# The last two attentions of a four-layer cross-attention kernel: attention outputs as products of high and low parts, values two steps ahead in shared places

## The chip, the cores and the metric

The kernel runs on one core of a Trainium2 chip. The metric is the device time of one execution in microseconds (us); lower is better.

## The reference

`x` is 8 x 256 x 256 (batch B=8, T=256 tokens, D=256), the context 8 x 64 x 256, all float32. Four cross-attention layers follow one another. The first three have small heads; the third ends in an MLP of width 1024. The fourth, called layer 3, holds two cross-attentions with 16 heads of K=128 and an MLP. Each of its attentions computes, with `h` the normalised `x`:

```python
qh = (h @ wq + bq).reshape(b, q_len, 16, 128)
kh = (kv @ wk + bk).reshape(b, 64, 16, 128)       # plus one more key row, bias_k
vh = (kv @ wv + bv).reshape(b, 64, 16, 128)       # plus one more value row, bias_v
weights = softmax(einsum('bqhk,bthk->bhqt', qh, kh) / sqrt(128))
x = x + einsum('bhqt,bthk->bqhk', weights, vh).reshape(b, q_len, 2048) @ wo + bo
```

After both, `x + gelu(layer_norm(x) @ w_fc1 + b_fc1) @ w_fc2 + b_fc2`.

## The kernel before

Each engine has its own hand-written instruction stream (functions `sync`, `tensor`, `vector`, `scalar`, `gpsimd`), and streams meet only at semaphores. A small class drops a wait whose value is already known to be reached on that engine. DMA loads are all issued by SyncE (SP), in order.

The two last attentions are one loop over steps, `STEPS` = -4 to 32. An attention is folded: since K=128 is as wide as the context is narrow, the kernel doesn't project queries. It multiplies the projected keys with wq, and the projected values with wo, per head. A tile is 128 tokens; there are 16 tiles in each attention, 32 in all, and `tile_of(j)` is tile j. Four tiles belong to a pair of batches, `n = j // 4`. Keys and values of a pair come in four quarters of four heads, `divmod(i, 4)`. In step j, quarter `j + 4` of the keys (`key_of`) and quarter `j + 3` of the values (`value_of`) are made, tile j gets scores and softmax, and tile j-1 its output. In even steps a later input is transposed.

TensorE (PE), in the order of a step: `key_projection` and `value_projection` (L866, from `project`), `tile_scores` (products of parts, L725 to L727), `key_products` (L943), `tile_transposed` of tile j-1 (L961), `value_products` (L979), `tile_output` of tile j-1 (L990), `tile_source` (L505, even steps). A float32 matmul is two records in the profile. "Products of parts": each float32 operand is held as a high part rounded to float32r and a low part, the rest; high x high, high x low and low x high are summed (`products`, L722). Scores already do so, outputs don't.

PSUM: the scores use two double banks, everything else four banks `work`, which change roles with each step (`step_banks`). A bank that holds value products in step j (third and fourth) is in step j+1 the one of the key projection (first) or value projection (second). `first_free` to `fourth_free` are the waits for that.

VectorE (DVE), in the order of a step: `value_bias` (L1486), in steps -4 to -1 `value_sums` (L1423), in steps 11 to 14 `wq_biased` (L1409), `tile_max_over` (L1502), `key_low` (L1494, two), `tile_shifted` (L1513), in steps 10 to 13 `wq_sums` (L1401), in even steps `tile_norm` (L1108), in steps 12 to 15 `value_sums` again, `tile_sums` (L1523 to L1527), in even steps `ln_finish` (L1118), `tile_residual` (L1533), in even steps `tile_source` (L1476, L1478), in steps -1 and 15 `value_constants` (L1539).

ScalarE (ACT): `key_bias` (L1899), `key_products` (high parts of the keys, L1909), `tile_out` of tile j-1 (transposed weights, L1929), `tile_exponentials` (L1922), `value_products` (L1917, plain float32 copies into `pv`). GpSimd (POOL): the statistics' small steps, the multiply of the exponentials by the reciprocals (L2166, after `tile_sums`), `wq_scaled` (L2141, after the multiply in steps 10 to 13), rows added to `x` (L2064). In step j, `wq_biased` waits for the `wq_scaled` of step j-1.

Keys live in 10 places of high and low parts, shared by quarter and batch, each used until its last tile's scores (`places_of_keys`). Values live in two buffers `pv`, one for each second pair. The keys' weights are streamed, 512 KB a step into two slots; the values' weights are loaded whole, four quarters an attention. `weight_high` (L1941, ACT) and `weight_low` (L2156, POOL) split the last MLP's weights in steps 28 and 29.

## Time and profile before

| | us |
|---|---|
| median of 3 runs | 1052.97 (1051.34 to 1053.47) |
| the profiled execution's own time | 1050.85 |
| its span | 1048.9 |
| PE busy | 983.2 (94%) |
| DVE busy | 710.6 (68%) |
| ACT busy | 515.1 (49%) |
| POOL busy | 402.8 (38%) |

The granted TensorE clock was 0.995 of full speed. The span runs from the first to the last instruction of the profiled execution; its own time holds 1.95 us more. A row of a timeline gives start, duration, engine, line, operation, output and input tiles, and in brackets how long the engine stood idle before it and what ended that. Busy times of PE are modelled and neighbours overlap, so spacings from start to start are the surer measure. PEld is the load of a matmul's stationary operand. The two attentions' loop lies between about 455 and 951 us of the span.

### The profile page before, as it was taken

What the parts mean: (1) busy time and instruction counts of PE and PEld (TensorE: products, weight loads), DVE (VectorE), ACT (ScalarE), POOL (GpSimd) and SP (SyncE); (2) the same over time, 40 slices, a digit from 0 to 9 for tenths busy, and PEclk for the clock granted to TensorE, in tenths of its full rate; (3) what the DMA queues carried; (4) which work ended last, traced back from release to release, by engine and by line L of the source; (5) the groups of instructions that cost most, each with busy time, mean ns of one, the idle gap of its engine ahead of it and who ended that gap; (6) DMA issues with size and microseconds to landing.
All of it is one profiled execution on the core that took longest, in us unless ns stands there. A gap on an engine that the chain in (4) does not pass through costs nothing.

```text
span 1048.9 us, 19279 instructions
## 1 busy us (share of the span) xinstructions
PE 983.2 (94%) x7764; PEld 829.5 (79%) x7764; DVE 710.6 (68%) x1199; ACT 515.1 (49%) x1028; POOL 402.8 (38%) x424
## 2 busy tenths in 40 slices
PE   6999999997998798988999999999999999989997
PEld 3667566555666798987898899889988899879997
DVE  4658999896788578645656667786566655675542
ACT  2557888777676544433333333333333433445542
POOL 2534689898876233100222213321222122362110
PEclk9999999999999999999999999999999999999999
DMA  9102000000000500041110024401110110200000
GB/s 328 61 1 81 1 2 1 2 1 2 1 1 1 207 15 1 1 139 43 42 41 32 30 82 141 140 22 41 41 39 23 41 41 2 81 1 11 22 21 31
DMA packets 23997, 47.57 MB, mean 45 GB/s; under 512 B 3938, under 2 KB 8804, under 8 KB 23268
## 3 DMA queue, kind: packets, MB, share of 16 engines
q1 hardware_dynamic: 23908, 46.34, 13.0%
q8 instruction: 61, 1.00, 0.4%
q14 instruction: 28, 0.23, 0.1%
HBM read 44.23 MB, written 2.10 MB: 44 GB/s over the span
## 4 chain that ended last, share of the span: by engine, by line
PE 72%; POOL 11%; DVE 9%; issue 4%; ACT 3%; DMA 0%; SPq 0%; POOLq 0%; DVEq 0%
PE work L990 10%; PE work L866 10%; PE work L979 5%; PE scores L725 5%; PE scores L727 5%; PE scores L726 5%; PE work L943 5%; POOL pair L2052 3%; PE work L725 3%; PE work L727 3%; PE work L726 3%; PE work L590 2%; PE work L961 2%; PE work L652 2%; POOL pair L2055 2%
## 5 line engine op out<-in xcount | busy, mean ns | idle before, releaser
L2011 POOL TENSOR_SCALAR stat<-stat 128x2 f32<-128x2 f32 (+1 forms) x49 | 11.1, 227 | 300.1 <-DVE stat L1112 298.8
L990 PE MATMUL work<-pair,probsT 128*128 128x256 f32 x512 | 119.1, 386 | 3.0 <-ACT probsT L1929 3.0
L866 PE MATMUL work<-ctxT,w 128*128 128x128 f32 x992 | 116.2, 275 | 3.3 <-DVE all_keys L1494 2.1
L866 PEld LDWEIGHTS work<-ctxT,w 128*128 128x128 f32 x992 | 114.5, 192 | 4.8 <-issue 4.0
L990 PEld LDWEIGHTS work<-pair,probsT 128*128 128x128 f32 x512 | 94.6, 190 | 26.3 <-issue 10.8
L1909 ACT ACTIVATE all_keys<-work 128x512 fp32r<-128x512 f32 x64 | 38.2, 597 | 143.1 <-PE work L943 143.1
L2166 POOL TENSOR_TENSOR probs<-probs,smax 128x1024 f32<-128x1024 f32 x22 | 42.0, 1909 | 139.0 <-DVE smax L1527 139.0
L1899 ACT ACTIVATE kvT<-work,cols 128x128 f32<-128x128 f32 x120 | 34.2, 368 | 106.0 <-PE work L866 106.0
L1502 DVE TENSOR_REDUCE smax<-scores 128x16 f32<-128x1024 f32 x32 | 39.1, 1222 | 53.9 <-PE scores L727 53.9
L725 PE MATMUL scores<-all_keys,src_l_high 128*128 128x256 f32 x256 | 74.5, 291 | 0.0
L727 PE MATMUL scores<-all_keys,src_l_low 128*128 128x256 f32 x256 | 71.7, 280 | 0.0
L726 PE MATMUL scores<-all_keys,src_l_high 128*128 128x256 f32 x256 | 71.6, 280 | 0.0
L979 PE MATMUL work<-w,kvT 128*64 128x256 f32 x512 | 62.3, 385 | 7.4 <-DVE all_keys L1494 7.4
L1174 DVE TENSOR_REDUCE smax<-scores 128x16 f32<-128x1024 f32 x48 | 58.1, 1210 | 11.6 <-PE scores L636 11.1
L1486 DVE TENSOR_TENSOR kvT<-work,cols 128x512 f32<-128x512 f32 x32 | 22.1, 690 | 63.5 <-PE work L866 63.5
L943 PE MATMUL work<-kvT,w 128*128 128x128 f32 x512 | 62.3, 275 | 0.0
L943 PEld LDWEIGHTS work<-kvT,w 128*128 128x128 f32 x512 | 59.8, 192 | 0.0
L979 PEld LDWEIGHTS work<-w,kvT 128*64 128x64 f32 x512 | 34.8, 136 | 25.9 <-issue 12.8
L1118 DVE TENSOR_SCALAR act_bufs<-x,stat 128x256 f32<-128x256 f32 x58 | 43.7, 796 | 16.1 <-POOL stat L2014 16.1
L2064 POOL TENSOR_TENSOR x<-x,rows_late 128x512 f32<-128x512 f32 x32 | 48.0, 1502 | 10.3 <-DVE act_bufs L1118 8.6
L2052 POOL TENSOR_TENSOR pair<-pair 128x512 f32<-128x512 f32 x32 | 41.3, 1289 | 27.2 <-ACT pair L1723 25.8
L1730 ACT ACTIVATE w<-work 128x512 f32<-128x512 f32 x88 | 47.3, 593 | 7.3 <-PE work L652 6.9
(198 smaller groups left out, 2802.8 us busy)
## 6 DMA issues: line engine op xcount, KB each, us to landing
w<-in_l_wk SPq DMA_DIRECT2D x32, 512.0 KB, 4.1
w<-in_l_wq SPq DMA_DIRECT2D x8, 512.0 KB, 5.9
w<-in_l_wo SPq DMA_DIRECT2D x8, 512.0 KB, 6.9
w<-in_l_wv SPq DMA_DIRECT2D x8, 512.0 KB, 4.3
x<-in_x SPq DMA_DIRECT2D x1, 2048.0 KB, 12.9
out<-x SPq DMA_DIRECT2D x8, 256.0 KB, 2.2
pair<-in_xT SPq DMA_DIRECT2D x1, 1536.0 KB, 7.1
pair<-in_l_fc SPq DMA_DIRECT2D x1, 1024.0 KB, 4.8
```

The lines of the kernel that those rows point to most:

```text
L725: mm(bank, s_hi, m_hi, start=start, stop=False)
L726: mm(bank, s_hi, m_lo, start=False, stop=False)
L727: return mm(bank, s_lo, m_hi, start=False, stop=stop)
L866: last = mm(bank[:, h * P:(h + 1) * P], w[:, c, h * K3:(h + 1) * K3], ctxT[:, c, p * P:(p + 1) * P], start=(c == 0), stop=(c == DC - 1))
L943: last = mm(step_banks(j)[2 + c][:, h * P:(h + 1) * P], w3_wq[:, 4 * g + h, c * P:(c + 1) * P], kvT[i % 2][:, h, :], start=True, stop=True)
L979: last = mm(bank[h * S:(h + 1) * S, bb * D:(bb + 1) * D], kvT[2][:, 2 * q + h, bb * S:(bb + 1) * S], w3_wo[:, 4 * g + 2 * q + h, :], start ...
L990: last = mm(step_banks(j + 1)[0][:, 0:D], probsT_bufs[j % 2][:, q, :], pv[n % 2][:, bb, q, :], start=(q == 0), stop=(q == GH // 2 - 1))
L1118: last = v.tensor_scalar(dst[:, t, :], src[:, t, :], st[:, 12 * t + 6:12 * t + 7], st[:, 12 * t + 9:12 * t + 10], ALU.subtract, ALU.mult)
L1174: v.tensor_reduce(smax[k % 2][:, 0:GH], s3, X, ALU.max).then_inc(d_max, 1)
L1730: act(pT[:, 4 * half:4 * half + 4, t, :], work[half][:, :].rearrange("p (q n) -> p q n", n=P), ACT.Copy).then_inc(a_pT, 1)
L2052: g.tensor_tensor(halves, e3[:, :, 0:n], e3[:, :, n:S], ALU.add).then_inc(p_half, 1)
L2064: g.tensor_tensor(xb(b), xb(b), row(name).unsqueeze(1).broadcast_to([P, TT, D]), ALU.add).then_inc(done, 1)
```

## The change

Each part as the code does it:

- `tile_output` uses products of parts. The transposed weights are held as high and low parts `pT_l3` in one buffer (before: whole, in two buffers), the values as high and low parts.
- Values get ten places of their own, assigned by the same function as the keys' places. Their high parts are written by ACT (`value_products`), their low parts by DVE (`value_low`, new). The low parts of the transposed weights are made by DVE (`tile_low`, new).
- Values are made two steps ahead, not three.
- The values' bias moves from DVE (one instruction) to ACT (four).
- The values' weights are streamed like the keys', a quarter at a time into two slots, 32 loads for 8.
- ACT copies values before the exponentials, not after. The last MLP's weights are split in steps 30 and 31 and lie elsewhere.

The pieces below come from the streams in this order: SP and PE, then DVE (`value_low`, `tile_low` and the loop), then ACT (`value_bias`, `value_products` and the loop).

```diff
         def value_of(j):
-            return j + 3 if 0 <= j + 3 < 8 * PAIRS else None
+            return j + 2 if 0 <= j + 2 < 8 * PAIRS else None
...
-            for i in range(4, 8 * PAIRS):
-                e.wait_ge(pe_kp, i - 1)
-                load_keys(i)
+            for i in range(2, 8 * PAIRS + 2):
+                if i < 8 * PAIRS:
+                    e.wait_ge(pe_kp, i - 1)
+                    load_quarter("k", i)
+                if i >= 4:
+                    e.wait_ge(pe_vp, i - 3)
+                    load_quarter("v", i - 2)
                 g = i - 2 - last
                 if 0 <= g < 4:
                     e.wait_ge(pe_pk, 2 * (last + g) + 2)
                     load_w3(2, g, "q")
-                if 1 <= g < 5:
-                    e.wait_ge(pe_pv, 2 * (last + g - 1) + 2)
-                    load_w3(2, g - 1, "vo")
+                if 2 <= g < 6:
+                    e.wait_ge(pe_pv, 2 * (last + g - 2) + 2)
+                    load_w3(2, g - 2, "o")
...
             def first_free(j):
                 e.wait_ge(d_mr, B)
                 e.wait_ge(d_kl, 2 * keys_before(j))
-                e.wait_ge(a_pv, 2 * values_before(j) - 1)
+                e.wait_ge(d_vl, 2 * values_before(j) - 1)
                 e.wait_ge(d_lr, tiles_before(j - 1))
             def second_free(j):
...
-                e.wait_ge(a_pv, 2 * values_before(j))
+                e.wait_ge(d_vl, 2 * values_before(j))
             def fourth_free(j):
...
-                e.wait_ge(d_vT, values_before(j))
-                e.wait_ge(a_lpT, 2 * tiles_before(j))
+                e.wait_ge(a_lv, values_before(j))
+                e.wait_ge(d_tl, 2 * tiles_before(j))
...
             def tile_output(j):
                 n, bb = j // 4, j // 2 % 2
-                e.wait_ge(a_lpT, 2 * j + 2)
-                e.wait_ge(a_pv, 8 * (n + 1))
                 for q in range(GH // 2):
-                    last = mm(step_banks(j + 1)[0][:, 0:D], probsT_bufs[j % 2][:, q, :], pv[n % 2][:, bb, q, :],
-                              start=(q == 0), stop=(q == GH // 2 - 1))
+                    e.wait_ge(d_tl, 2 * j + q // 4 + 1)
+                    e.wait_ge(d_vl, 8 * n + q + 1)
+                    k = value_at[PLACES[n, q // 2][bb]]
+                    last = products(step_banks(j + 1)[0][:, 0:D], [v[:, q, :] for v in pT_l3],
+                                    [all_values[:, k + part, q % 2, :] for part in range(2)], q == 0, q == GH // 2 - 1)
                 last.then_inc(pe_lo, 1)
...
-            def value_bias(i):
-                a, n, g = attention_of(i)
-                e.wait_ge(pe_vp, i + 1)
-                e.wait_ge(d_diff, 4)
-                e.wait_ge(pe_pv, 2 * i)
-                v.tensor_tensor(kvT[2][:, :, :], step_banks(i - 3)[1][:, :].rearrange("p (h s) -> p h s", h=4),
-                                col(f"l3_bv{a}", 4 * g, 4).unsqueeze(2).broadcast_to([P, 4, P]),
-                                ALU.add).then_inc(d_vT, 1)
+            def value_low(i):
+                for q in range(2):
+                    e.wait_ge(a_pv, 2 * i + q + 1)
+                    v.tensor_tensor(both_values(i, q, 1), step_banks(i - 2)[2 + q][:, :].rearrange("p (b d) -> p b d", b=2),
+                                    both_values(i, q, 0).bitcast(F32), ALU.subtract).then_inc(d_vl, 1)
+            def tile_low(j):
+                for half in range(2):
+                    high, low = (flat(p[:, 4 * half:4 * half + 4, :]) for p in pT_l3)
+                    e.wait_ge(a_lpT, 2 * j + half + 1)
+                    v.tensor_tensor(low, step_banks(j + 1)[half][:, :], high.bitcast(F32), ALU.subtract).then_inc(d_tl, 1)
...
             for j in STEPS:
-                if value is not None:
-                    value_bias(value)
                 if j < 0:
                     value_sums(1, j + 4)
                 if 11 <= j < 15:
                     wq_biased(2, j - 11)
                 if tile_of(j) is not None:
                     tile_max_over(j)
                 if key_of(j) is not None:
                     key_low(key_of(j))
+                if j == 4 * B:
+                    hidden_low(0, 0)
+                    last_affine(1)
+                    hidden_low(0, 1)
+                if tile_of(j - 1) is not None:
+                    tile_low(j - 1)
                 if tile_of(j) is not None:
                     tile_shifted(j)
+                if value_of(j) is not None:
+                    value_low(value_of(j))
...
+            def value_bias(i):
+                a, n, g = attention_of(i)
+                e.wait_ge(pe_vp, i + 1)
+                e.wait_ge(d_diff, 4)
+                e.wait_ge(pe_pv, 2 * i)
+                for h in range(4):
+                    last = act(kvT[2][:, h, :], step_banks(i - 2)[1][:, h * P:(h + 1) * P], ACT.Identity,
+                               bias=col(f"l3_bv{a}", 4 * g + h))
+                last.then_inc(a_lv, 1)
             def value_products(i):
-                a, n, g = attention_of(i)
-                slot_free(n, pe_lo, None)
+                e.wait_ge(d_mr, B)
+                e.wait_ge(pe_lo, PLACES[divmod(i, 4)][2])
                 for q in range(2):
                     e.wait_ge(pe_pv, 2 * i + q + 1)
-                    act(pv[n % 2][:, :, 2 * g + q, :],
-                        step_banks(i - 3)[2 + q][:, :].rearrange("p (b d) -> p b d", b=2), ACT.Copy).then_inc(a_pv, 1)
+                    act(both_values(i, q, 0), step_banks(i - 2)[2 + q][:, :].rearrange("p (b d) -> p b d", b=2),
+                        ACT.Copy).then_inc(a_pv, 1)
...
                 if key is not None:
                     if key >= 2:
                         key_bias(key)
+                if value is not None:
+                    value_bias(value)
+                if key is not None:
                     key_products(key)
...
+                if value is not None:
+                    value_products(value)
                 if tile_of(j) is not None:
                     tile_exponentials(j)
-                if value is not None:
-                    value_products(value)
-                if j in (4 * B - 4, 4 * B - 3):
+                if j in (4 * B - 2, 4 * B - 1):
                     for q in range(4):
-                        weight_high(j - 4 * B + 4, q)
+                        weight_high(j - 4 * B + 2, q)
```

## Rows read from the trace of the kernel before

**Rows 1.** The page's part 1, busy us, share of span, instructions.

```profile
PE 983.2 (94%) x7764; PEld 829.5 (79%) x7764; DVE 710.6 (68%) x1199; ACT 515.1 (49%) x1028; POOL 402.8 (38%) x424
```

**Rows 2.** Windows of steps 17 and 11: stretch, its length, busy times, clock, DMA.

```profile
743.00:757.60 14.60, 14.60 (x114) 13.20 (x114) 6.75 (x11) 5.35 (x11) 1.90 (x1) 1.00 0.11 36
646.00:661.00 15.00, 15.00 (x118) 13.55 (x117) 14.47 (x27) 5.36 (x11) 5.82 (x4) 1.00 0.43 141
```

**Rows 3.** Timeline of PE, from step 14's value products into step 15.

```profile
701.58 1.95 PE L979 MATMUL work<-w,kvT 128*64 128x256 f32 x16
703.46 3.72 PE L990 MATMUL work<-pair,probsT 128*128 128x256 f32 x16
707.02 0.60 PE L505 MATMUL work<-ident,act_bufs 128*128 128x128 f32 x4
...
710.95 0.37 PE L725 MATMUL scores<-all_keys,src_l_high 128*128 128x256 f32 x1
...
713.86 1.95 PE L943 MATMUL work<-kvT,w 128*128 128x128 f32 x16
```

**Rows 4.** Timeline of step 16, DVE and PE's outputs, to step 17's maximum.

```profile
729.08 1.22 DVE L1502 TENSOR_REDUCE smax<-scores 128x16 f32<-128x1024 f32 x1 [2.14 <-PE scores L727]
...
731.49 0.69 DVE L1494 TENSOR_TENSOR all_keys<-work,all_keys 128x512 fp32r<-128x512 f32 x1 [0.20 <-ACT all_keys L1909]
732.10 1.21 DVE L1513 TENSOR_TENSOR probs<-scores,smax 128x1024 f32<-128x1024 f32 x1
...
733.50 3.72 PE L990 MATMUL work<-pair,probsT 128*128 128x256 f32 x16
...
734.53 1.22 DVE L1523 TENSOR_REDUCE smax<-probs 128x16 f32<-128x1024 f32 x1 [0.26 <-ACT probs L1922]
...
739.36 0.69 DVE L1478 SCALAR_TENSOR_TENSOR src_l_low<-work,src_l_high 128x512 fp32r<-128x512 f32 x1
...
744.09 1.23 DVE L1502 TENSOR_REDUCE smax<-scores 128x16 f32<-128x1024 f32 x1 [2.12 <-PE scores L727]
```

**Rows 5.** Timeline of DVE, POOL and PE in steps 10 to 14.

```profile
638.36 1.22 DVE L1502 TENSOR_REDUCE smax<-scores 128x16 f32<-128x1024 f32 x1 [2.13 <-PE scores L727]
...
646.71 2.23 DVE L1118 TENSOR_SCALAR act_bufs<-x,stat 128x256 f32<-128x256 f32 x2
...
646.87 1.92 POOL L2166 TENSOR_TENSOR probs<-probs,smax 128x1024 f32<-128x1024 f32 x1 [0.58 <-DVE smax L1527]
...
648.75 2.41 POOL L2141 TENSOR_TENSOR w<-w,pair 128x1024 f32<-128x1024 f32 x1
...
651.19 2.30 DVE L1409 TENSOR_TENSOR w<-w,pair 128x1024 f32<-128x1024 f32 x1
653.41 1.21 DVE L1502 TENSOR_REDUCE smax<-scores 128x16 f32<-128x1024 f32 x1
...
667.96 1.22 DVE L1502 TENSOR_REDUCE smax<-scores 128x16 f32<-128x1024 f32 x1 [0.99 <-PE scores L727]
...
684.83 1.21 DVE L1502 TENSOR_REDUCE smax<-scores 128x16 f32<-128x1024 f32 x1
...
686.16 1.28 DVE L1494 TENSOR_TENSOR all_keys<-work,all_keys 128x512 fp32r<-128x512 f32 x2
...
686.99 1.95 PE L979 MATMUL work<-w,kvT 128*64 128x256 f32 x16 [1.39 <-DVE all_keys L1494]
...
698.23 1.23 DVE L1409 TENSOR_TENSOR w<-w,pair 128x1024 f32<-128x1024 f32 x1 [1.33 <-POOL w L2141]
699.37 1.22 DVE L1502 TENSOR_REDUCE smax<-scores 128x16 f32<-128x1024 f32 x1
```

**Rows 6.** The page's part 6, DMA issues: count, KB each, us to landing.

```profile
w<-in_l_wv SPq DMA_DIRECT2D x8, 512.0 KB, 4.3
```

**Rows 7.** Timeline of PE, the opening of step -2.

```profile
466.89 3.81 PE L866 MATMUL work<-ctxT,w 128*128 128x128 f32 x32
```

**Rows 8.** Timeline of PE, step 31's transposes.

```profile
934.44 1.09 PE L961 MATMUL work<-ident,probs 128*128 128x128 f32 x8 [1.46 <-POOL probs L2166]
```

More of the change, by code:

```diff
@@ L133, in build @@
         probsT_sb = sb("probsT", [P, GH, P])
-        probsT_bufs = [probsT_sb[:, 8 * i:8 * i + 8, :] for i in range(2)]
+        probsT_at = nc.sbuf_base - 4 * GH * P
         smax = [sb(f"smax{i}", [P, 48]) for i in range(2)]
@@ L379, in both_keys, with both_values @@
             return all_keys[:, a:b + 1:b - a, c, :].rearrange("p b (h k) -> p b h k", h=4)
+        def both_values(i, q, part):
+            first, second, _ = PLACES[divmod(i, 4)]
+            a, b = value_at[first] + part, value_at[second] + part
+            return all_values[:, a:b + 1:b - a, q, :]
         def attention_of(i):
```

124 lines of the change are left out of this document (54 added, 70 removed).

## The prediction

> **What bounds the kernel now.** I read the page first, then windows of one step each, then the PE and DVE timelines, and last the steps with extra work. A step is one of the 37 passes of the last attentions' loop (j = -4 to 32), named by the tile j whose scores it makes. PE is busy 94% of the span and DVE 68% [rows 1]. In an ordinary step PE is busy all of it and DVE about half; in step 11 DVE is busy 14.5 of 15.0 us [rows 2], and in step 13 PE waits 1.39 us for it [rows 5]. So PE bounds the ordinary steps, and DVE is close to it in steps 10 to 15. PE's order in a step, to be followed in the timeline: two projections (L866), scores (L725), key products (L943), transposes, value products (L979), outputs (L990) and, in even steps, an input's transposes (L505) [rows 3]. The steps open with L866, 0.43 after L505 has begun. From maximum to maximum an even step takes 15.02 us (729.08 to 744.09 [rows 4]) and an odd one 14.58; 29.60 for two.
>
> **The outputs on PE.** Eight full-width matmuls run from 703.46 to 707.02: 3.56 us [rows 3]. They become 24 part products of the form that the scores have, 128x128 by 128x256, and 24 of those take 710.95 to 713.86, 2.91 us [rows 3]. Gain 0.65 us a tile. Its lower bound is nothing, if parts cost as much as whole ones, its upper 0.74, if the 0.09 of the change of type were not paid. I take 0.65, since the row is of the same form. PE alone would so need 13.93 and 14.37 us, 28.30 for two.
>
> **What DVE gets.** Two subtractions for the output parts of the values (value_low) and two for the transposed weights (tile_low), less one bias add. The nearest row is a pair of key_low, the same shapes: 1.28 us for two (L1494 at 686.16 [rows 5]), a little less from start to start; I take 1.25, so 2.5 before the row sums end, and 0.6 off in front of the next maximum. In an ordinary even step DVE's last operation ends at 740.0, and the next maximum waits for PE till 744.09: 4.1 us free [rows 4]. Less 2.5, less 0.65 (PE comes earlier), plus a 0.26 wait for the exponentials which goes: 1.2 us stay free. So there it costs nothing, and the cover is the scores of the next step; without it each us would be lost once in two steps.
>
> **New waits.** (1) The next key projection waits for value_low's first half, whose bank it overwrites. Counted from the maximum's start: key_low ends at 3.0 (729.08 to 732.10), tile_low 4.25, the shift 5.5, first half 6.1, and 0.13 more to reach PE (686.16 and 0.69 against 686.99 [rows 5]): 6.25. PE opens the outputs at 4.4 (733.50 [rows 4]) and arrives 2.9 later: 7.3. Free: 1.1 us. Behind the wait stands all of PE. (2) The outputs wait for tile_low, done at 3.7 for the first half; PE is there at 4.4. (3) With values two steps ahead the last quarter of a pair is made in the step that first reads it. Its halves are wanted at 6.5 and 6.9 and done at 6.25 and 6.9: I take nothing, bounds 0 and 0.4 in each of 7 steps.
>
> **Edits at nothing, in ordinary steps.** ScalarE's bias, four instructions, lies between the value projection's end and the key products, about 2.3 us of cover; uncovered it costs 1.1 a step. The value weights' loads add 512 KB a step (36 GB/s becomes about 70; in step 11 141 GB/s stand beside a full PE [rows 2]); they are queued behind the key's on SP, leave after a value projection two steps before their use, 28 us, and land in 4.3 us [rows 6]; without that cover each would cost up to 4.3. The places are shared in the keys' pattern and free in time. The MLP's weight parts move from steps 28 and 29 to 30 and 31, under the last chain and the hidden layer.
>
> **Steps 10 to 15, the term that decides.** Here DVE also has wq_sums (1.6), wq_biased and value_sums (2.0), and wq_biased(j) waits for POOL, whose multiply and scaling start only after the row sums. So 2.5 us before the sums move POOL, wq_biased and the next maximum alike. Maximum 10 to 11: sums end at 646.71 - 638.36 = 8.35, now 10.85; POOL's two 4.3 (646.87 to 651.16) after 0.16; then wq_biased 2.2: 17.55, where PE's share is 14.4 [rows 5]. The same way from the other starts (653.41, 667.96, 684.83, 699.37), estimates: 11 to 12: 15.5; 12 to 13: 19.15; 13 to 14: 17.05; 14 to 15: 14.65, there DVE's own queue; 15 to 16: 15.85, since the one matmul on value_sum waits until these sums are done. Together 99.75. Before they were 729.08 - 638.36 = 90.7 [rows 4, 5]. So +9.0, where PE alone would have given -5.4. Each late maximum makes key_low late, and the value products wait for key_low, as they already did in step 13 (1.39 us at 686.99).
>
> One price there stands both ways in the rows: wq_biased takes 2.30 us beside a POOL operation and 1.23 without, where it had waited 1.33 us for POOL [rows 5]. By the Trainium skill (SBUF — State Buffer, "SBUF: two separate sides") a DVE operation with two SBUF inputs and a GpSimd one that reads SBUF exclude each other, and whichever starts first holds the port. By that rule wq_biased could win twice (steps 11 and 13) and the sum would be 2.2 us lower than mine, which keeps 2.2 us for it there.
>
> **Start and end.** Start: with no value work in step -3, key projection 2 waits only for key_low(1), at 464.9 instead of 466.89 [rows 7]: -1.9. In steps -2 to 0 the projections wait for value_low, but ScalarE then takes the values before the exponentials, and step 1 opens at 496.1 instead of 498.7; -3.1 at step 2's start, with its tile's 0.65. Bounds 0 and -5. End: from step 28 to the hidden layer 39.8 us before. Step 29 gets a projection and products (1.77 + 1.87), four outputs give 2.6 back, and tile_low now stands between a maximum and its shift, in a part where PE waits for POOL's multiply anyway (1.46 at 934.44 [rows 8]): +0.6, bounds -3 and +4.
>
> **Sum.** Start -3.1; steps 2 to 9, 8 x -0.65 = -5.2; maxima 10 to 16 +9.0; the 12 steps 16 to 27 -7.8; end +0.6. Together -6.5. The profiled execution took 1050.85 (its span 1048.9, 1.9 around it), so 1044.4; it lies 2.1 under the median of the three timed runs, 1052.97. Carried to the median: 1046.5.
>
> **Rivals.** (A) The forecast: PE gains, and half of it is given back in steps 10 to 15: 1046.5, by itself 1041 to 1051. Chance 0.50. (B) No pile-up: the extra work slips into DVE's idle time, as its busy sum allows (14.5 of 15.0 us in step 11, half in ordinary steps). Then 14.4 of the term goes: 1032. Against it: in-order waits on POOL, which busy sums don't show. Chance 0.15. (C) Slower: the bank release of wait (1). It has 1.1 us free, and four subtractions, two evictions and a shift stand in its chain. If each step's chain is longer by d, about 27 steps lose d - 1.1; from d = 1.43 the kernel is slower than before, at d = 1.75 it is 1064. For it: a second key_low already waits 0.2 for ScalarE [rows 4], and there are more such hand-overs now. Against: four of them make 0.8. Chance 0.12. (D) The pile-up is larger than 14.4, as late maxima also delay the inputs' sources and the last quarter of values in step 13, and it reaches on into steps 16 and 17: 20 to 25 of it leaves 1052 to 1057. Chance 0.20. (E) The change doesn't do what it says, outputs as parts cost as much as whole: 28 x 0.65 lost, 1064.7. Chance 0.03; the scores' rows speak against it.
>
> About 0.2% (2.1 us) can be told from no change here. Faster by more: A but for a sliver, B, a little of D: 0.66. Within: most of D's better half and a sliver of A: 0.16. Slower: C, E and the rest of D: 0.18. The range leaves out the far half of B, most of C, and E: 1034 to 1057.
>
> **What would show it.** Right: no L990-like full matmuls; output groups of 2.9 us; ordinary steps of 13.9 and 14.4 us, with PE full and DVE at about 11 us of 14; maxima 10 to 16 spread over some 100 us with PE waiting for key_low before the value products, 1 to 5 us at a time in steps 11 to 14; step 1 opening some 2.6 us earlier. Wrong: PE waiting for value_low before a key projection in every step (C), for tile_low before the outputs, maxima 10 to 16 in 86 us (B), or a projection waiting for a DMA.

## The result, and the profile after

| | before | after |
|---|---|---|
| median of 19 runs each, us | 1051.27 | 1047.32 (1044.67 to 1051.02) |
| the profiled execution's own time | 1050.85 | 1046.57 |
| its span | 1048.9 | 1044.8 |
| granted TensorE clock | 0.995 | 0.989 |

The ratio is 0.9966, 95% interval [0.9955, 0.9976]: the changed kernel is faster by 3.9 us. Of its 19 executions the eleven with a granted clock of 0.987 to 0.990 took 1044.67 to 1047.80 us and the eight with 0.983 or 0.984 took 1048.39 to 1051.02, and the profile below is of the first kind. The forecast time, 1046.5, is 0.8 under the median. Of the forecast gain of 6.5 only 3.9 to 4.1 came, though: the three timed runs of before from which it was carried had a median 1.7 us above that of the 19 runs since.

The page of the changed kernel, busy times, and the streamed values' weights, 32 loads where [rows 6] has 8:

```profile
PE 969.0 (93%) x8020; PEld 827.6 (79%) x8020; DVE 758.1 (73%) x1295; ACT 558.0 (53%) x1156; POOL 403.6 (39%) x424
...
w<-in_l_wv SPq DMA_DIRECT2D x32, 512.0 KB, 5.0
```

Against [rows 1], PE is busy 14 us less while the span is only 4.1 shorter: some 10 us of new idle time stand in it. The waits of PE say where (who waits for whom, us in total, times, longest):

```profile
PE work L989 <- DVE all_keys L1496: 12.1, 7, 3.0
...
PE work L876 <- DVE all_keys L1496: 6.2, 1, 6.2
...
PE work L735 <- DVE pT_l_low L1510: 5.1, 3, 2.5
```

The code has moved down by some lines: the projections are L876 (before L866), products of parts L735 to L737 (L725 to L727; those with `pT_l` as operand are the new outputs), key products L953, transposes L971, value products L989, the maximum L1517, `key_low` L1496, `value_low` L1502, `tile_low` L1510, `wq_biased` L1420, `wq_scaled` L2161. L989 in the first line is so the wait of the value products, not an output.

**Ordinary steps.** PE's timeline, openings of steps 5 to 8, and the window of steps 5 and 6 (length, then PE, PEld, DVE, ACT, POOL busy, clock, DMA share, GB/s):

```profile
567.84 3.74 PE L876 MATMUL work<-ctxT,w 128*128 128x128 f32 x32
...
582.22 3.74 PE L876 MATMUL work<-ctxT,w 128*128 128x128 f32 x32
...
596.16 3.74 PE L876 MATMUL work<-ctxT,w 128*128 128x128 f32 x32
```

```profile
567.84:596.16 28.32, 28.32 (x246) 26.34 (x245) 20.83 (x37) 13.46 (x30) 6.08 (x5) 1.00 0.24 76
```

14.38 and 13.94 us, 28.32 for two, where 28.30 was forecast. PE is busy all of it and DVE for 20.8 of 28.3. In step 16 DVE has 1.38 us free before step 17's maximum, where the prediction kept 1.2:

```profile
743.40 1.22 DVE L1517 TENSOR_REDUCE smax<-scores 128x16 f32<-128x1024 f32 x1 [1.38 <-PE scores L737]
```

An output is now the stretch between L735 at 508.28 and L876 at 511.20, 2.92 us, where it was 3.56 [rows 3]:

```profile
508.28 0.38 PE L735 MATMUL work<-all_values,pT_l_high 128*128 128x256 f32 x1
...
511.20 3.07 PE L876 MATMUL work<-ctxT,w 128*128 128x128 f32 x26
```

**Steps 10 to 16.** DVE's timeline, the first three and the last of the seven maxima (the brackets tell for how long DVE had been idle, and for what):

```profile
631.07 1.22 DVE L1517 TENSOR_REDUCE smax<-scores 128x16 f32<-128x1024 f32 x1 [5.28 <-PE scores L737]
648.52 1.21 DVE L1517 TENSOR_REDUCE smax<-scores 128x16 f32<-128x1024 f32 x1
663.48 1.22 DVE L1517 TENSOR_REDUCE smax<-scores 128x16 f32<-128x1024 f32 x1
...
729.03 1.23 DVE L1517 TENSOR_REDUCE smax<-scores 128x16 f32<-128x1024 f32 x1 [4.96 <-PE scores L737]
```

97.96 us from 10 to 16, against 90.7 before [rows 4, 5]; those between are at 682.24, 699.14 and 713.53. The chain that stretches them, step 10 into step 11, on three engines:

```profile
641.63 0.25 DVE L1542 RECIPROCAL smax<-smax 128x16 f32<-128x16 f32 x1
641.96 1.92 POOL L2186 TENSOR_TENSOR probs<-probs,smax 128x1024 f32<-128x1024 f32 x1 [0.58 <-DVE smax L1542]
643.85 2.43 POOL L2161 TENSOR_TENSOR w<-w,pair 128x1024 f32<-128x1024 f32 x1
646.23 1.28 POOL L2084 TENSOR_TENSOR x<-x,rows_late 128x512 f32<-128x512 f32 x1
646.31 2.29 DVE L1420 TENSOR_TENSOR w<-w,pair 128x1024 f32<-128x1024 f32 x1 [0.62 <-POOL w L2161]
...
650.59 1.95 PE L989 MATMUL work<-w,kvT 128*64 128x256 f32 x16 [2.52 <-DVE all_keys L1496]
```

Multiply and scaling on POOL, then `wq_biased` on DVE, then the maximum, `key_low`, and only then the value products, for which PE has waited 2.52 us. In this profile the clock stayed at 1.00 behind that wait. In four other profiles with the same code in these steps (f3, f4, g2 and h1 below) the 16 value products behind the waits of 2.5 us (step 11) and 2.8 us (step 13) took 3.3 to 3.6 us each time instead of 1.95, and the seven maxima spanned 99.0 to 99.4 us; in f2 they spanned 97.94, at full clock.

**Where the gain went.** How far each mark lies ahead of the same mark of before (us), and what was forecast:

| mark | before | after | ahead | forecast |
|---|---|---|---|---|
| maximum 10 | 638.36 | 631.07 | 7.3 | 8.3 |
| maximum 16 | 729.08 | 729.03 | 0.05 | -0.7 |
| step 28 opens | 900.07 | 892.35 | 7.7 | 7.1 |
| hidden layer begins | 939.64 | 934.88 | 4.8 | 6.5 |
| end of the span | 1048.9 | 1044.8 | 4.1 | 6.5 |

All that was won up to maximum 10 is gone at maximum 16, the next twelve steps win 7.7 again, and the last four steps give 3.0 back where 0.6 was forecast.

**The last four steps.** Timeline of step 31 in the changed kernel, and the window of its outputs:

```profile
926.03 1.09 PE L971 MATMUL work<-ident,probs 128*128 128x128 f32 x8 [0.27 <-POOL probs L2186]
926.47 1.22 DVE L1517 TENSOR_REDUCE smax<-scores 128x16 f32<-128x1024 f32 x1
927.65 4.97 POOL L2176 TENSOR_TENSOR w_low<-w,w_high 128x512 fp32r<-128x512 f32 x4
927.73 1.21 DVE L1519 TENSOR_SCALAR smax<-smax 128x16 f32<-128x16 f32 x1
928.86 1.28 DVE L1510 TENSOR_TENSOR pT_l_low<-work,pT_l_high 128x512 fp32r<-128x512 f32 x2
929.59 0.58 PE L735 MATMUL work<-all_values,pT_l_high 128*128 128x256 f32 x1 [2.47 <-DVE pT_l_low L1510]
...
934.88 0.41 PE L735 MATMUL scores<-src_high,w_high 128*128 128x256 f32 x1
```

```profile
929.50:934.80 5.30, 5.21 (x24) 5.21 (x25) 3.55 (x7) 3.35 (x6) 3.58 (x4) 0.50 0.00 0
```

Between the transposes and the outputs PE waits 2.47 us for `tile_low`, which stands behind the maximum and the small operation L1519; that one took 1.21 us instead of the 0.18 it takes elsewhere. Then the granted clock is 0.50, the lower level of 1.2 GHz, and the 24 products take 5.29 us instead of 2.92. From the transposes to the hidden layer it is 8.85 us, against 5.20 before (934.44 [rows 8] to 939.64). Whether the clock falls here changes from profile to profile, as the experiments show.

**The start.** The same happens in step -2; PE's timeline and a window:

```profile
465.01 5.25 PE L876 MATMUL work<-ctxT,w 128*128 128x128 f32 x32 [6.24 <-DVE all_keys L1496]
```

```profile
465.00:468.00 3.00, 2.99 (x14) 3.00 (x15) 1.71 (x4) 0.00 (x0) 0.00 (x0) 0.50 0.00 0
```

The projection starts at 465.0 (forecast 464.9), but with nothing left for PE in step -3 its two waits of 2.1 us have become one of 6.24, the clock is 0.50 behind it, and 32 matmuls take 5.25 us. Before, they took 3.81 [rows 7].

### The profile page after: what moved, and what is told of

Same layout as the page of the kernel before. It is cut to its first block, busy times and chain, and to the rows that moved or that the text cites. A ratio compares the mean times of both kernels' runs of the same rounds, so it can differ in the third digit from the quotient of the medians.

```text
span 1044.8 us, 20014 instructions
## 1 busy us (share of the span) xinstructions
PE 969.0 (93%) x8020; PEld 827.6 (79%) x8020; DVE 758.1 (73%) x1295; ACT 558.0 (53%) x1156; POOL 403.6 (39%) x424
## 4 chain that ended last, share of the span: by engine, by line
PE 64%; DVE 14%; POOL 13%; issue 5%; ACT 3%; DMA 0%; POOLq 0%; SPq 0%; DVEq 0%
PE work L876 9%; PE work L735 6%; PE work L737 5%; PE work L736 5%; PE scores L735 5%; PE scores L737 5%; PE scores L736 5%; PE work L989 5%; PE work L953 4%; POOL pair L2072 4%; PE work L600 2%; POOL pair L2075 2%; PE work L971 2%; PE work L662 2%; PE work L515 1%
## 5 line engine op out<-in xcount | busy, mean ns | idle before, releaser
L876 PE MATMUL work<-ctxT,w 128*128 128x128 f32 x992 | 117.7, 277 | 6.5 <-DVE all_keys L1496 6.2
L876 PEld LDWEIGHTS work<-ctxT,w 128*128 128x128 f32 x992 | 114.9, 194 | 7.5 <-issue 7.5
L1517 DVE TENSOR_REDUCE smax<-scores 128x16 f32<-128x1024 f32 x32 | 39.1, 1223 | 82.3 <-PE scores L737 82.1
L735 PE MATMUL work<-all_values,pT_l_high 128*128 128x256 f32 x256 | 76.2, 297 | 5.1 <-DVE pT_l_low L1510 5.1
L735 PE MATMUL scores<-all_keys,src_l_high 128*128 128x256 f32 x256 | 74.1, 290 | 0.0
L989 PE MATMUL work<-w,kvT 128*64 128x256 f32 x512 | 62.3, 385 | 12.1 <-DVE all_keys L1496 12.1
L737 PE MATMUL work<-all_values,pT_l_low 128*128 128x256 f32 x256 | 72.8, 285 | 0.0
L736 PE MATMUL work<-all_values,pT_l_high 128*128 128x256 f32 x256 | 72.8, 284 | 0.0
L737 PE MATMUL scores<-all_keys,src_l_low 128*128 128x256 f32 x256 | 71.7, 280 | 0.0
L953 PE MATMUL work<-kvT,w 128*128 128x128 f32 x512 | 62.8, 275 | 1.1 <-DVE x L1548 0.9
L735 PEld LDWEIGHTS work<-all_values,pT_l_high 128*128 128x128 f32 x256 | 49.2, 192 | 17.0 <-DVE pT_l_low L1510 17.0
L953 PEld LDWEIGHTS work<-kvT,w 128*128 128x128 f32 x512 | 59.9, 192 | 1.6 <-issue 1.1
L989 PEld LDWEIGHTS work<-w,kvT 128*64 128x64 f32 x512 | 34.6, 136 | 30.9 <-issue 10.7
L1935 ACT ACTIVATE all_values<-work 128x512 fp32r<-128x512 f32 x64 | 38.3, 598 | 31.7 <-PE work L989 31.7
```

Source lines behind the costliest of these rows:

```text
L735: mm(bank, s_hi, m_hi, start=start, stop=False)
L736: mm(bank, s_hi, m_lo, start=False, stop=False)
L737: return mm(bank, s_lo, m_hi, start=False, stop=stop)
L876: last = mm(bank[:, h * P:(h + 1) * P], w[:, c, h * K3:(h + 1) * K3], ctxT[:, c, p * P:(p + 1) * P], start=(c == 0), stop=(c == DC - 1))
L953: last = mm(step_banks(j)[2 + c][:, h * P:(h + 1) * P], w3_wq[:, 4 * g + h, c * P:(c + 1) * P], kvT[i % 2][:, h, :], start=True, stop=True)
L989: last = mm(bank[h * S:(h + 1) * S, bb * D:(bb + 1) * D], kvT[2][:, 2 * q + h, bb * S:(bb + 1) * S], w3_wo[:, 4 * g + 2 * q + h, :], start ...
```

## Experiments

Every one starts from the changed kernel. Ratios are against the kernel before as timed beside the experiment, with 95% intervals; its medians there were 1051.23 us (f1 to f4), 1051.30 (g1 to g4) and 1051.97 (h1 to h3).

### The bias product behind the low parts (f1_bias_late)

Theory: in steps 11 to 14 the chain POOL, `wq_biased`, maximum is the bound, since `wq_biased` stands in front of the maximum.

```diff
-                if 11 <= j < 15:
-                    wq_biased(2, j - 11)
                 if tile_of(j) is not None:
                     tile_max_over(j)
...
                 if value_of(j) is not None:
                     value_low(value_of(j))
+                if 11 <= j < 15:
+                    wq_biased(2, j - 11)
```

> The changed kernel with wq_biased of steps 11 to 14 moved on DVE from before the maximum to behind value_low. Theory (the pile-up is an order, not a shortage: the row sums, POOL's multiply and scaling, wq_biased and the maximum form one chain): the span between maxima 10 and 16 falls from 97.96 us to about 92 (intervals 14.7, 13.9, 17.5, 13.9, 15.9, 15.9), the kernel gets about 6 us faster than the changed kernel. Rival (DVE is simply full there, its work takes as long wherever it stands): the maxima keep within 2 us of 98, nothing gained.

Measured 1042.20 us, ratio 0.9911 [0.9896, 0.9927], 5.1 under the changed kernel. Its first maxima of that stretch, and PE's wait:

```profile
634.33 1.23 DVE L1517 TENSOR_REDUCE smax<-scores 128x16 f32<-128x1024 f32 x1 [5.29 <-PE scores L737]
648.87 1.22 DVE L1517 TENSOR_REDUCE smax<-scores 128x16 f32<-128x1024 f32 x1
662.86 1.23 DVE L1517 TENSOR_REDUCE smax<-scores 128x16 f32<-128x1024 f32 x1 [2.60 <-PE scores L737]
```

```profile
PE work L989 <- DVE all_keys L1496: 3.7, 4, 1.5
PE work L953 <- DVE x L1548: 2.5, 2, 2.1
```

The intervals are now 14.54 and 13.99 us, where they were 17.45 and 14.96, and the seven maxima span 93.36 (634.33 to 727.69): 4.6 us are back, of the 7.2 that the stretch had lost. PE's wait for `key_low` falls from 12.1 to 3.7, and DVE no longer waits for POOL at `wq_biased` (9.3 us before the move). A wait of the key products takes its place, 2.05 us in step 13: they wait for tile 11's residual (L1548), whose bank they overwrite, and that comes at the end of step 12, where DVE is busy for 16.99 of 17.49 us. So the position of this one operation is the cause of most of the 7.2 us. Measured against PE alone (three times 28.32, 84.96 us) the changed kernel's 97.96 lie 13.0 over, and 8.4 of that are left. Most of them stand in steps 12 and 14 (17.49 and 16.82 us), which DVE's own work fills: it is busy for 16.99 and 16.58 us of them.

A second effect of the move can be read off. Each `wq_biased` now takes 1.22 us, where two had taken 2.29 and 2.30 beside a POOL operation; that is 2.1 us less. But the small operation behind the maximum meets POOL instead, in three steps, and takes 0.69, 0.65 and 1.47 us for 0.17:

```profile
696.72 1.47 DVE L1519 TENSOR_SCALAR smax<-smax 128x16 f32<-128x16 f32 x1
```

DVE's busy time over the seven maxima stayed the same (82.5 us, before the move 82.2), so the gain is in the waits and not in this price.

### The low parts before the last maximum (f2_low_first)

```diff
+                if j == 4 * B - 1:
+                    tile_low(j - 1)
                 if tile_of(j) is not None:
                     tile_max_over(j)
...
-                if tile_of(j - 1) is not None:
+                if tile_of(j - 1) is not None and j != 4 * B - 1:
                     tile_low(j - 1)
```

> In step 31 tile_low of tile 30 stands on DVE before the maximum instead of behind it. Theory (the wait of 2.47 us before tile 30's outputs lets TensorE's clock fall to half, which doubles the time of the 24 products that follow): the outputs start about 1.5 us earlier, the clock stays at 1.0 and they take 2.9 us, so the hidden layer begins about 3.9 us earlier. Rival (only the wait counts): 1.5 us earlier, and the products still at half speed.

Measured 1046.32 us, ratio 0.9960 [0.9946, 0.9974]; the profile shows the step better than the medians do. PE in its step 31:

```profile
927.86 0.38 PE L735 MATMUL work<-all_values,pT_l_high 128*128 128x256 f32 x1 [0.97 <-DVE pT_l_low L1510]
932.67 0.36 PE L735 MATMUL scores<-src_high,w_high 128*128 128x256 f32 x1 [1.72 <-POOL w_low L2178]
```

The wait for `tile_low` is 0.97 instead of 2.47, the clock stays at 1.00, and PE is done with the outputs 5.2 us after the transposes' start (925.79). But the hidden layer then waits 1.72 us for POOL's low parts of its weights, which the slow outputs had covered. From transposes to hidden layer 6.88 instead of 8.85: 2.0 us less, not 3.9. These 2.0 can't be credited to the edit alone. f1 and h3 leave `tile_low` behind the maximum and have the wait of 2.46 and 2.47 us, but in their profiles the clock stayed at 1.00, and they too need 6.88 and 6.90; their hidden layer waits 0.21 and 0.25 us for POOL. At full clock POOL's split of the weights so ends this interval at 6.9 us with either order.

### Work for PE in the same wait (f3_filler)

```diff
+                if j == 4 * B - 1:
+                    for _ in range(10):
+                        mm(work[1][:, 0:P], ident[:, :], ones[:, :], start=True, stop=True)
                 if tile_of(j - 1) is not None:
                     tile_output(j - 1)
```

> Ten extra matmuls of ident by ones (2.2 us) into a free half bank stand on PE between tile 30's transposes and its outputs, where PE waits 2.47 us for tile_low; they take nothing away from the wait. Theory (idle time makes the clock fall): the outputs begin where they did but run at full speed, 2.9 us instead of 5.3; 2.4 us faster than the changed kernel. Rival (the clock falls in that stretch for another reason, such as a throttle of the whole core): outputs still at half speed, nothing gained.

Measured 1046.81 us, ratio 0.9951 [0.9933, 0.9970]. PE in step 31, and the window in which the outputs run:

```profile
928.80 2.40 PE L1091 MATMUL work<-ones,ident 128*128 128x128 f32 x20
931.45 0.39 PE L735 MATMUL work<-all_values,pT_l_high 128*128 128x256 f32 x1 [0.26 <-DVE pT_l_low L1513]
...
934.77 0.36 PE L735 MATMUL scores<-src_high,w_high 128*128 128x256 f32 x1 [0.19 <-POOL w_low L2179]
```

```profile
931.00:933.00 2.00, 1.74 (x15) 1.55 (x15) 2.00 (x3) 0.00 (x0) 2.00 (x2) 1.00 0.00 0
```

The outputs start as late as before, and they run at full clock. From transposes (927.87) to hidden layer 6.90 us, 1.95 less. So of the loss in this step about 2 us are the clock. That PE's idleness brings them about is not shown by this run: without extra work the same wait of 2.46 to 2.48 us was followed by 8.85 to 8.86 us in three profiles (the changed kernel's, g2, h1), 7.95 in f4, where the clock came back after about half of the outputs, and 6.88 and 6.90 in f1 and h3. The filler's 6.90 can be the filler's doing or such a draw.

### The values' sums late at the start (f4_sums_late)

The value sums of quarters 1 to 3, on DVE in steps -3 to -1 ahead of `key_low`, go to the end of step -3.

```diff
-                if j < 0:
-                    value_sums(1, j + 4)
+                if j == -4:
+                    value_sums(1, 0)
...
+                if j == -3:
+                    for q in range(1, 4):
+                        value_sums(1, q)
                 if j in (-1, 15):
```

> At the loop's start the value_sums of steps -3 to -1 move behind key_low, all to the end of step -3. Theory: key projection 2 no longer waits 2.0 us for a value_sums that stands ahead of key_low(1), and the clock falls later or not at all, so step 1 opens 3 to 4 us earlier than the changed kernel's 497.2. Rival (key_low there waits for POOL's statistics, and the later steps of the start wait for value_low anyway): step 1 opens within 1 us of 497.2.

Measured 1045.10 us, ratio 0.9941 [0.9928, 0.9953]. Its opening of step -2:

```profile
465.27 6.12 PE L876 MATMUL work<-ctxT,w 128*128 128x128 f32 x32 [4.28 <-DVE all_keys L1496]
```

PE waits 4.28 us instead of 6.24, but the clock falls behind this wait as well: the projection takes 6.12 us. From step -3's key products (457.26) to step 1 (497.23) it is 39.97 us, in the changed kernel 42.15 (455.04 to 497.19). That is 2.2 us, between the two numbers on record, and the clock hides a part of it: to the next key products the projection needs 5.96 us here and 5.08 in the changed kernel. Without the projection's own time 34.01 us are left for 37.07 (and 34.02 in g3, which has the same edit), so the order wins 3.1 us, as the theory had it.

### Only the high parts of the outputs (g1_high_only)

The low parts are made but not multiplied, so this kernel leaves their share of the outputs out. It shortens PE by 16 of 24 products a tile, to see which new wait comes first.

```diff
-                    last = products(step_banks(j + 1)[0][:, 0:D], [v[:, q, :] for v in pT_l3],
-                                    [all_values[:, k + part, q % 2, :] for part in range(2)], q == 0, q == GH // 2 - 1)
+                    last = mm(step_banks(j + 1)[0][:, 0:D], pT_l3[0][:, q, :], all_values[:, k, q % 2, :],
+                              start=(q == 0), stop=(q == GH // 2 - 1))
```

> The changed kernel, but PE makes of each tile's outputs only the high by high product: 8 matmuls for 24; all low parts are still made. (Left out: the low parts' share of the outputs.) PE alone would then need 12.0 and 12.5 us for an odd and an even step. Theory (the release of value_low's bank, 6.25 us after the maximum's start, comes next, 6.6 after a step's opening): ordinary steps settle at about 12.85 us odd and 13.2 even, some 26.0 for two against 28.3, and PE waits for value_low before the key projection. Rival 1 (the release has room for more than that): 24.5 for two. Rival 2 (DVE was already the bound of ordinary steps): 28 for two, nothing gained.

Measured 1027.36 us, ratio 0.9770 [0.9751, 0.9789]. PE's waits of that kind, and the opening of an ordinary step:

```profile
PE work L1001 <- DVE all_values L1502: 7.9, 16, 0.9
PE work L876 <- DVE all_values L1502: 7.3, 19, 1.2
```

```profile
732.27 3.81 PE L876 MATMUL work<-ctxT,w 128*128 128x128 f32 x32 [0.18 <-DVE all_values L1502]
```

Steps open at 732.27, 745.91 and 758.76: 26.49 us for two. That is 1.83 less than 28.32, where 16 products of 0.117 us less in each would give 3.7; waits (1) and (3) of the prediction have taken the other half. The projection waits for `value_low` 19 times, the outputs for the last quarter (here L1001) 16 times. In the changed kernel both are covered, by some 0.9 us a step (half of 1.83; the prediction had 1.1): a chain longer than that, and rival C would have begun.

### The streamed values' weights twice (g2_loads_twice)

```diff
                     load_quarter("v", i - 2)
+                    a, _, g = attention_of(i - 2)
+                    e.wait_ge(s_in[f"l3_wv_{i % 2}"], 16 * 2 * ((i - 2) // 2))
+                    nc.sync.dma_start(w3_wv[:, i % 2, :, :],
+                                      A[f"l3_wv{a}"].rearrange("p (c n) -> p c n", c=DC)[:, :, 4 * g * K3:(4 * g + 4) * K3]
+                                      ).then_inc(s_in[f"l3_wv_{i % 2}"], 16)
...
-                e.wait_ge(s_in[f"l3_wv_{i % 2}"], 16 * (i // 2 + 1))
+                e.wait_ge(s_in[f"l3_wv_{i % 2}"], 16 * (2 * (i // 2) + 1))
```

> Each streamed quarter of the values' weights from the third on is loaded twice, the second time after the first has landed; projections wait for both. Theory (loads are hidden two steps ahead): ordinary steps stay at 13.93 and 14.37 us, the time within 1 us of the changed kernel's. Rival (traffic or SP's queue costs something in each step): at least 0.1 us a step, 3 us together, with waits of PE for a DMA.

Measured 1046.61 us, ratio 0.9963 [0.9949, 0.9977], the changed kernel's own time. Two steps of it:

```profile
740.90:769.20 28.30, 28.30 (x246) 26.33 (x245) 20.81 (x37) 13.47 (x30) 6.04 (x6) 1.00 0.34 113
```

113 GB/s and 28.30 us, against 76 GB/s and 28.32 above. The second loads cost nothing, and no wait of PE for a load of these weights appears.

### The three moves together (g3_three)

f1, f2 and f4 in one kernel.

> wq_biased behind value_low, value_sums late at the start and tile_low first in step 31, together. Theory (three separate stretches, gains add up): -4.6 in steps 10 to 15, -2.2 at the start, -2.0 at the end, 8.8 us less than the changed kernel's 1047.3, about 1038.5. Rival (the end's gain goes to the wait for POOL's weight_low, which then decides when the hidden layer starts): about 1040.5.

Measured 1039.49 us, ratio 0.9886 [0.9866, 0.9905]: between the two numbers, and faster than both kernels by 11.8 and 7.8 us. Maxima 10 to 16 span 92.89 us (630.04 to 722.93), step 1 opens 39.29 us after step -3's key products, and the hidden layer still waits for POOL:

```profile
926.79 0.36 PE L735 MATMUL scores<-src_high,w_high 128*128 128x256 f32 x1 [1.68 <-POOL w_low L2181]
```

### The last weights split earlier (g4_four)

To take that last wait, three of the first weight's four low parts go ahead of POOL's multiply in step 30 (its high parts ahead of the exponentials; the lines for that, and those that leave them out at the old places, are not printed).

```diff
+                if j == 4 * B - 2:
+                    for q in range(3):
+                        weight_low(0, q)
                 if tile_of(j) is not None:
```

> As the three together, and ScalarE makes the high parts of w1 before the exponentials of step 30, POOL three of four low parts before its multiply there. Theory (the hidden layer waits 1.72 us for weight_low once tile_low comes first): that wait goes, 1.5 us less than the three, about 1037. Rival (POOL's port keeps DVE's small operations of step 30 waiting and its multiply comes later): no gain or up to 2 us slower than the three.

Measured 1040.75 us, ratio 0.9895 [0.9877, 0.9913]: no gain on g3, though the intervals overlap. The wait moved to the transposes, which need POOL's multiply, and the clock fell again:

```profile
921.62 1.09 PE L971 MATMUL work<-ident,probs 128*128 128x128 f32 x8 [1.91 <-POOL probs L2197]
...
923.69 0.58 PE L735 MATMUL work<-all_values,pT_l_high 128*128 128x256 f32 x1 [0.98 <-DVE pT_l_low L1510]
```

```profile
923.60:929.00 5.40, 5.31 (x25) 5.32 (x26) 4.20 (x7) 2.06 (x4) 0.92 (x1) 0.50 0.00 0
```

The outputs take 5.28 us here for 2.92 at full clock. From the last scores of step 31 to the hidden layer it is 9.55 us in g4 and 7.45 in g3 (from 919.42 and 919.34). Without the 2.4 us of the clock the two would be about level, an estimate from these rows. So POOL's late multiply, the rival's reason, takes back what the earlier split gives, and the rest of the loss in this profile is the clock.

### Work for PE in the start's wait (h1_start_filler, h2_three_filler)

```diff
+                if j == -2:
+                    for _ in range(24):
+                        mm(sc[1][:, 0:P], ident[:, :], ones[:, :], start=True, stop=True)
                 if key is not None and key >= 2:
                     key_projection(j, key)
```

> The changed kernel with 24 plain float32 matmuls of ones in front of step -2's key projection, into a score bank that nothing uses at that time (they add nothing to the result). They fill most of the 6.24 us in which PE waits there for the keys' low parts. Theory: the projection's 32 matmuls took 5.25 us because the clock had fallen to 0.50 in the wait; with PE kept at work the clock stays at 1.00 there, they take about 3.75, and step 1 opens about 1.5 us earlier (40.6 instead of 42.15 after step -3's key products). Median down by about 1.5, to 1045.8. Rival: the steps behind are set by DVE and ScalarE, so step 1 opens as before and the time stays.

Measured 1047.09 us, ratio 0.9953 [0.9930, 0.9976], which can't be told from the changed kernel's 0.9966. The timeline shows the difference:

```profile
457.24 3.74 PE L953 MATMUL work<-kvT,w 128*128 128x128 f32 x32
460.81 5.52 PE L1074 MATMUL scores<-ones,ident 128*128 128x128 f32 x48
467.21 3.81 PE L876 MATMUL work<-ctxT,w 128*128 128x128 f32 x32 [0.87 <-DVE all_keys L1499]
```

The projection starts 9.97 us after step -3's key products, as it did (455.04 to 465.01), and takes 3.81 us at a clock of 1.00. Step 1 opens at 497.96, 40.72 after the key products instead of 42.15: 1.43 us, as the theory had it. Here the other profiles bear the theory out. In all ten without it the clock fell behind the wait of 6.24 or 4.28 us, and the projection needed 5.0 to 6.5 us to the next key products (5.08 in the changed kernel's, 4.99 in f2, 6.53 in f1); with it, here and in the next kernel, 3.65. The rest of the way to step 1 was 27.1 us in each profile with the changed kernel's start. So the clock costs 1.3 to 2.9 us there, and the changed kernel's profile has nearly the least of it. All of this profile lies 2.2 us later from before this loop on (457.24 against 455.04), in a part that the edit doesn't touch; shifts of that size can hide 1.4 us in a median of eight.

The same in the kernel of the three moves, with 17 matmuls:

> The kernel of the three moves (keys' bias product late, values' sums late, the last low parts first), with 17 such matmuls in front of step -2's key projection. Theory: the clock holds there as well, and some 1.5 us go from the 39.3 us between step -3's key products and step 1: 1038.0. Rival: no change, 1039.5.

Measured 1038.45 us, ratio 0.9871 [0.9851, 0.9892], the lowest time here; 0.9886 was g3's ratio. Step 1 opens 38.17 us after the key products (457.04 to 495.21), 1.1 less than in g3; the medians differ by 1.0, and the intervals overlap. In step 30 of this profile the clock fell in the middle of the outputs, behind waits of only 0.78 and 0.98 us, where g3 has the same waits and kept 1.00.

### The values' bias back on DVE (h3_bias_dve)

```diff
+                if value_of(j) is not None:
+                    value_bias(value_of(j))
                 if j < 0:
                     value_sums(1, j + 4)
```

(and ScalarE's call taken out; `value_bias` is DVE's single instruction of before.)

> The changed kernel with the values' bias back on DVE, one instruction at the front of its step, as before the change. Theory: in ordinary steps DVE has over 1 us free and nothing changes; in steps 10 to 15, where DVE's own queue sets the maxima, 0.6 us a step comes back, about 3 for the 97.96 of maxima 10 to 16; at the start, DVE has the key sums too: up to 1. Together 1050 to 1051. Rival: wq_biased waits for POOL anyway, so the bias add slips into that wait and costs nothing: 1047.3.

Measured 1048.58 us, ratio 0.9971 [0.9955, 0.9987]. The intervals from maximum 10 to 15 are 17.46, 14.97, 18.75, 16.89 and 14.98 us, in the changed kernel 17.45, 14.96, 18.76, 16.90 and 14.39. Where DVE waits for POOL anyway the bias add costs nothing; only 14 to 15, DVE's own queue, grows by 0.59. The rival was right for steps 10 to 13. At the start it costs more: step 1 opens 45.10 us after step -3's key products (457.88 to 502.98) instead of 42.15, and 1.4 of these 2.95 are the clock, with a projection of 6.62 us. That part isn't the edit's: f1, f3, g1 and g2 have the changed kernel's start and about as slow a projection (6.1 to 6.5 us to the next key products, here 6.45). The bias add costs the other 1.6.

This kernel's step 31, like f1's, gave something that no edit was meant for. It has the changed kernel's code there and the same wait, but not its clock:

```profile
935.90 0.39 PE L735 MATMUL work<-all_values,pT_l_high 128*128 128x256 f32 x1 [2.47 <-DVE pT_l_low L1519]
...
939.23 0.36 PE L735 MATMUL scores<-src_high,w_high 128*128 128x256 f32 x1 [0.25 <-POOL w_low L2185]
```

```profile
935.80:939.20 3.40, 3.08 (x24) 2.88 (x25) 2.26 (x5) 1.43 (x2) 3.17 (x3) 1.00 0.00 0
```

From transposes (932.33) to hidden layer 6.90 us, to the hundredth what the filler gave.

## Why the prediction was right, and where it was off

**The outputs: right.** 2.92 us a tile for a forecast 2.91, and 28.32 for two steps where PE alone should need 28.30. Rival E is out.

**What DVE gets, and waits (1) to (3): right.** In step 16 the first half of `value_low` (735.14, from the row at 734.45 and one eviction of 0.69) is done 6.1 us after the maximum, as worked out; PE doesn't wait for it in ordinary steps, and g1 shows both slacks to be small and real. The 1.2 us that were to stay free on DVE were 1.38. Rival C had the right place and did not reach its price.

**Edits at nothing: right but for one.** g2 shows it for the loads. The bias on ScalarE is no cost, and h3 shows what it saves: 0.59 in the one interval that DVE's own queue sets, and 1.6 at the start. The edit that was not free is the move of the MLP's weight parts; it comes under the end.

**Steps 10 to 15: the mechanism right, the size 1.8 too large in this profile.** Forecast, interval by interval, 17.55, 15.5, 19.15, 17.05, 14.65 and 15.85; measured 17.45, 14.96, 18.76, 16.90, 14.39 and 15.50. Each is 0.1 to 0.55 shorter than its estimate; that instructions summed at full durations overlap a little at their starts would do this, but it wasn't tried by itself. In f3, f4, g2 and h1, where the clock fell twice in these steps, the same seven maxima span 99.0 to 99.4, within 0.8 of the forecast 99.75. That nearness is luck, since the forecast had no clock in it. The pile-up over PE alone is 13.0 us here and up to 14.4 there, forecast 14.4, so rival D with its 20 to 25 is out. (The "-5.4" for PE alone is itself rough: three times 28.30 is 84.9, which makes it -5.8.) f1 shows that `wq_biased` in front of the maximum, in the chain through POOL, caused 4.6 us of the stretch; what is left is DVE's own work. Rival B, that idle time on DVE would absorb the work, is out: DVE was busy for 82 of these 98 us, and its in-order waits for POOL made up most of the rest (9.3 us in four). On the port, the changed kernel has `wq_biased` at 2.29 us in step 11, where POOL's addition had started 0.08 us earlier (646.23 and 646.31), and at 2.30 in step 13. By the Trainium skill (SBUF — State Buffer, "SBUF: two separate sides") whichever of the two starts first holds the port; the trace agrees, and it was POOL in both, so the 2.2 that this rule could have given were rightly kept in the sum.

**The start: one step of it failed.** "At 464.9 instead of 466.89" came to the tenth. "Step 1 opens at 496.1" didn't: 497.19. The difference is a term that the sum didn't have, the clock behind the 6.24 us wait that the change itself makes by emptying step -3. h1 gives 1.43 us for it in this profile, and up to 2.9 stood in others. (2.6 earlier at step 1 and the tile's 0.65 make -3.25, where the sum has -3.1.)

**The end: mis-sized.** The term "+0.6, bounds -3 and +4" measured +3.0. It named `tile_low` between a maximum and its shift and put it "in a part where PE waits for POOL's multiply anyway". That cover was gone: POOL's multiply ended early (wait 0.27), and `tile_low` instead stood behind the maximum, with POOL's weight split moved into the same 5 us. From transposes to hidden layer it was 3.65 more (8.85 for 5.20): 1.73 from the wait of 2.47 where before the outputs waited 0.74 for ScalarE, and 1.95 from the clock (f1, f3 and h3 are without it). Up to the transposes the last steps had won 0.7. The move of the weights to steps 30 and 31, costed at nothing, is the step that I should have followed: DVE's L1519 ends only when POOL's first subtraction does, a microsecond late, and once the outputs run at full clock the split ends last itself (f1, f2, f3, g3, h3). So 1.7 of the 3.65 stay even where the clock doesn't fall.

**Why 3.9 and not 6.5.** In the profile, start +1.0, steps 10 to 15 -1.8, end +2.4, and +0.7 behind the hidden layer's start, which stays unexplained (109.26 us before, 109.92 after; with the clock at 1.00 instead of 0.98 it was 107.97 in h3 and 108.02 in f1). The clock is what the sum left out in more than one place: the granted clock of the whole span fell from 0.995 to 0.989, a part of it in the start and the end here; other profiles have it in steps 11 and 13 too. The forecast time came nearer to the measured one than its own sum deserved, by the 1.7 us of the three-run median: from 1051.27 the forecast gain would have given 1044.8, 2.5 under the measured time. So much of the hit was luck.

## What to carry to other kernels

When a change adds work to an engine that is not the bound, look for the steps in which that engine also waits for a third one. Idle time at such a wait takes new work only where the third engine doesn't wait for that work: the bias add of h3, placed behind the row sums and ahead of the wait, cost nothing in steps 11 to 13, while the 2.5 us placed ahead of the row sums moved the whole chain. An operation with a slack of its own, such as a bias product not needed before the next key products, belongs behind the operations that the bound engine waits for. And when a change leaves the bound engine without work for a few us, price the clock after the wait, not only the wait, and read more than one profile, since the same wait may be followed by either clock.

## What the runs showed of the hardware

- TensorE's granted clock fell to 0.50 (1.2 of 2.4 GHz) behind the waits of 6.24 and 4.28 us in step -2, in all ten profiles without work for PE there; the 32 matmuls of the projection, 3.65 us at full clock from start to start, took 5.0 to 6.5. With PE kept at work in the wait it stayed at 1.00, both times. At the lower clock products start 0.21 us apart instead of 0.117.
- Behind shorter waits it fell in some profiles and not in others of the same code. Behind 2.46 to 2.48 us in step 31 the outputs ran at 0.50 in three profiles, in part in one and at 1.00 in two (8.85 to 8.86, 7.95, 6.88 and 6.90 us to the hidden layer). Behind 2.5 and 2.8 us in steps 11 and 13 the value products took 3.3 to 3.6 us in four profiles and 1.95 in two. In f1, with a wait of 2.05 us up to 679.25, the granted clock was 0.85 from 679 to 682 us and 0.59 from 682 to 685; in g4 it was 0.50 behind waits of 1.91 and 0.98 us, and in step 30 of h2 it fell behind 0.78 and 0.98. By the Trainium skill (TensorE: Matmul & The Clock Gate, "What's actually happening") the gate judges activity by a schedule of its own, which doesn't start with the kernel; these profiles agree with that, though no run here shows the schedule. So one profile with or without such a dip is not proof that an edit caused or cured it; a wait that is gone is.
- A small DVE operation, L1519 with 128 x 16 elements, ended with the POOL operation on two SBUF operands that it met. In step 31 it took 1.21 us instead of 0.18 beside POOL's subtractions (4.97 us for four); in f1 it took 0.69, 0.65 and 1.47 us and ended 0.03 to 0.04 us behind POOL's operation each time. DVE's subtractions with an operand in PSUM kept their 1.28 us for two.
